# A one-layer language-model tower: the prologue's lists in another order, and VectorE's select of an expert unit ahead of the maximum

## The reference

```python
h = embeddings[x]                                   # one-hot product
n = layernorm(h)
q, k, v = n @ w_qkv  # 16 heads of 16; q and k are rotated (rope)
h = h + softmax(q @ k.T * 16 ** -0.5) @ v @ w_proj
y = layernorm(h)
e = argmax(y @ gate_w.T)                            # one of 8 experts per token
out = h + y + y @ expert_w[e].T
```

## Time and profile before

| | |
|---|---|
| median of 3 runs | 310.07 us (309.95 to 310.33) |
| profiled execution | 309.91 us, span 308.1 us |
| TensorE busy | 280.6 us, 91% |
| VectorE busy | 246.1 us, 80% |
| ScalarE busy | 132.8 us, 43% |
| GpSimd busy | 84.6 us, 27% |
| mean granted TensorE clock | 0.989 |

### The profile page before, as it was taken

The page is one execution under the profiler, slowest core; times in us unless marked ns, Lnnn a source line. Parts: engine busy times, 40 slices in busy tenths (PEclk is TensorE's granted clock), DMA queues, the critical chain, the costliest instruction groups (busy, mean ns, idle before and its releaser), DMA issues.

```text
span 308.1 us, 5610 instructions
## 1 busy us (share of the span) xinstructions
PE 280.6 (91%) x2060; PEld 200.9 (65%) x2060; DVE 246.1 (80%) x602; ACT 132.8 (43%) x271; POOL 84.6 (27%) x96
## 2 busy tenths in 40 slices
PE   2878889898799999899998999899999999999895
PEld 2657656656566776577766776677666666667674
DVE  8797997688969699788987798779897874657765
ACT  3155427667655535353436442463543454331000
POOL 5735418254454023411231041301210210210210
PEclk9999995999999999999999999999999999999999
DMA  3430331912900750049001930166010010001010
GB/s 117 179 150 7 110 105 47 152 26 62 150 8 12 127 81 2 12 103 138 4 0 39 155 52 1 36 115 94 2 37 3 2 36 2 1 3 34 0 36 34
DMA packets 10803, 17.55 MB, mean 57 GB/s; under 512 B 2024, under 2 KB 4883, under 8 KB 10648
## 3 DMA queue, kind: packets, MB, share of 16 engines
q1 hardware_dynamic: 9988, 16.62, 26.4%
q0 software_dynamic: 768, 0.55, 0.7%
q10 hardware_dynamic: 20, 0.02, 0.0%
HBM read 5.30 MB, written 2.10 MB: 24 GB/s over the span
## 4 chain that ended last, share of the span: by engine, by line
PE 52%; DVE 30%; issue 8%; POOL 5%; ACT 4%; DVEq 0%; POOLq 0%
PE e_bank L473 14%; PE f_bank L473 7%; PE o_bank L638 7%; DVE neg_max L986 6%; DVE acc L1083 5%; PE t_pair L603 5%; PE s_pair L473 4%; POOL qk L394 3%; PE m_bank L473 3%; PE s_pair L573 2%; PE m_bank L652 2%; DVE rope_a L969 2%; DVE rope_b L973 2%; ACT probs L850 2%; DVE xn L951 1%
## 5 line engine op out<-in xcount | busy, mean ns | idle before, releaser
L850 ACT ACTIVATE probs<-t_pair 128x512 f32<-128x512 f32 x128 | 69.6, 595 | 85.1 <-PE t_pair L603 84.6
L986 DVE TENSOR_REDUCE neg_max<-s_pair 128x2 f32<-128x512 f32 x128 | 81.9, 682 | 13.7 <-PE s_pair L573 13.5
L573 PE MATMUL s_pair<-stacks 48*128 48x256 f32 x256 | 49.4, 314 | 1.0 <-DVE neg_max L986 0.7
L603 PE MATMUL t_pair<-stacks 50*128 50x256 f32 x256 | 47.5, 313 | 1.9 <-DVE neg_max L986 1.4
L603 PEld LDWEIGHTS t_pair<-stacks 50*128 50x128 f32 x256 | 33.6, 189 | 23.8 <-issue 21.4
L473 PE MATMUL e_bank<-ew_h,y_h 128*128 128x512 f32 x92 | 40.3, 438 | 4.6 <-DVE acc L1079 2.7
L1083 DVE SCALAR_TENSOR_TENSOR acc<-e_bank,mask,acc 128x256 f32<-128x256 f32 x66 | 28.8, 478 | 11.2 <-PE e_bank L473 10.7
L573 PEld LDWEIGHTS s_pair<-stacks 48*128 48x128 f32 x256 | 34.6, 189 | 3.5 <-DVE neg_max L986 2.1
L473 PE MATMUL e_bank<-ew_l,y_h 128*128 128x512 f32 x92 | 36.4, 396 | 0.0
L473 PE MATMUL e_bank<-ew_h,y_l 128*128 128x512 f32 x92 | 36.2, 394 | 0.0
L394 POOL TENSOR_TENSOR qk<-rope_a,rope_b 128x512 f32<-128x512 f32 x16 | 20.6, 1294 | 54.2 <-DVE rope_b L973 54.2
(11 more groups left out here) (174 smaller groups left out, 536.6 us busy)
## 6 DMA issues: line engine op xcount, KB each, us to landing
stacks<-parts SPq DMA_DIRECT2D x36, 256.0 KB, 6.2
ew_raw<-in_expert_w SPq DMA_DIRECT2D x1, 2048.0 KB, 8.2
out<-res SPq DMA_DIRECT2D x7, 256.0 KB, 2.1
stacks<-parts SPq DMA_DIRECT2D x12, 128.0 KB, 2.9
probs<-in_w_qkv SPq DMA_DIRECT2D x2, 384.0 KB, 3.7
stacks<-max_rows SPq DMA_DIRECT2D x30, 8.0 KB
h<-in_emb,ids POOLq DMA_INDIRECT x16, 2.6
probs<-in_w_proj SPq DMA_DIRECT2D x1, 256.0 KB, 2.8
```

Source lines behind the costliest of these rows:

```text
L573: m = mm(s_pair[:, half, t * N:(t + 1) * N], stacks[b % STACKS][r:r + KS, pair, 0, t * P:(t + 1) * P], stacks[b % STACKS][r:r + KS, pair, ...
L603: m = mm(t_pair[:, half, c * N:(c + 1) * N], stacks[b % STACKS][r:r + KM, pair, 1, c * P:(c + 1) * P], stacks[b % STACKS][r:r + KM, pair, ...
L850: nc.scalar.activation(probs[:, (2 * v + half) % RING, :, :].rearrange("p c n -> p (c n)"), t_pair[:, half, :], ACT.Exp, scale=SCALE).then ...
L986: v.tensor_reduce(neg_max[:, k // 4, :, 4 * half + k % 4], s_pair[:, half, :].rearrange("p (t n) -> p t n", t=NT), AX.X, ALU.max, negate=T ...
```

## The change

On VectorE the select of a unit stands at the head of its slot, ahead of the maximum of that slot. In the prologue, VectorE makes f_norm_a(1) and x_low(0) ahead of the memsets of vals, subtracts y_l (x_low(1)) ahead of the z list and turns z_low and z_again round; the memsets of the ones column come last. ScalarE copies two z banks of the second tile (s_pair) ahead of two of the first, and the values of v later. GpSimd gathers batch 3 before it splits weights. TensorE's v projections are cut in two and moved behind visits 3 to 6, both transposes of batch 1 come a visit sooner, the first transpose of maxima goes into t_pair (`first_max_transpose`), one chunk of q and k moves behind visit 0 of step 0, and the fills there change from 2 ahead of step 0 and 1 after each of its visits to 3 after visit 0, 4 after visit 1 and 1 after each of the others.

```diff
@@ -219,7 +219,7 @@
             return (y_h[0], y_l[0]) if k == 1 else (x_h, x_l)
 
         Z_BANKS = [[m_bank, o_bank, f_bank, e_bank], [s_bank[0], s_bank[1], m_bank, o_bank]]
-        Z_ORDER = [(t, q) for t in range(NT) for q in range(4)]
+        Z_ORDER = [(0, 0), (0, 1), (1, 0), (1, 1), (0, 2), (0, 3), (1, 2), (1, 3)]
 
         def z_copied(t, q):
 
@@ -455,9 +455,9 @@
             rotated_sum(1, 0)
             rotated_sum(1, 1)
             f_rs_of(2)
+            gather(3)
             gate_weights()
             proj_weights_low()
-            gather(3)
             steps(step)
 
 
@@ -491,18 +491,21 @@
                         m = tr(x_bank(b)[:, k:k + P], xn[:, t, c * P:(c + 1) * P], ident[:, :])
                 m.then_inc(xt_ps, 1)
 
-            def project_v(b):
-                if b >= 2:
+            def project_v(b, tiles=range(NT)):
+                if tiles[0] > 0:
+                    pass
+                elif b >= 2:
                     wait(pe, qkl_ok, (b - 1) * NT + NT)
                 elif b == 1:
                     wait(pe, v_ok, b)
                 else:
                     pe.wait_ge(z_in, z_copied(1, 3))
                 x_h, x_l = x_parts(b)
-                for t in range(NT):
+                for t in tiles:
                     m = product(v_bank(b)[:, t * D:(t + 1) * D], lambda c: x_h[:, c, t, :], lambda c: x_l[:, c, t, :],
                                 lambda c: wqkv_h[:, c, 2 * D:3 * D], lambda c: wqkv_l[:, c, 2 * D:3 * D])
-                m.then_inc(v_ps, 1)
+                if tiles[-1] == NT - 1:
+                    m.then_inc(v_ps, 1)
 
             def project_qk(b, t, parts=range(C)):
                 if parts[0] > 0:
@@ -575,10 +578,19 @@
                 if t == NT - 1:
                     m.then_inc(s_ps, 1)
 
+            def first_max_transpose():
+
+                pe.wait_ge(roped, 2 * 2 * NT)
+                pe.wait_ge(ml_ok, 1)
+                for t in range(NT):
+                    m = tr(t_bank[1][0:16, N + t * P:N + (t + 1) * P].bitcast(F32R),
+                           max_parts[:, 0, t, :, :, :].rearrange("p i a j -> p (i a j)"), ident_r[:, :])
+                m.then_inc(mt_ps, 1)
+
             def max_transpose(b, u):
 
                 wait(pe, o_ok, (b - 1) * GROUPS + (4 if u else 2))
-                if b == 0 and u == 0:
+                if b == 0:
                     pe.wait_ge(v_ok, 2)
                 wait(pe, ml_ok, b * 2 + u + 1)
                 for t in range(NT):
@@ -712,8 +724,11 @@
                     g_at = SLOTS * b + s
                     if s % 2 == 0:
                         visit(b, s // 2)
+                        if b == 0 and s == 0:
+                            project_qk(2, 1, [1])
+                            pe.wait_ge(xl_ok, 3)
                         if b == 0:
-                            fill(m_bank, 1)
+                            fill(m_bank, 3 if s == 0 else 4 if s == 2 else 1)
                     if here(b, 0) and s == 3:
                         max_transpose(b, 1)
                     if here(b, 1) and s == maxima_slot(b + 1):
@@ -772,25 +787,24 @@
             project_qk(1, 1)
             z_transpose(1)
             visit(-1, 0)
-            project_v(0)
+            qk_transpose(1, 0)
             visit(-1, 1)
-            qk_transpose(1, 0)
+            qk_transpose(1, 1)
             visit(-1, 2)
-            qk_transpose(1, 1)
             x_transpose(2)
             visit(-1, 3)
-            project_v(1)
+            project_v(0, [0])
+            first_max_transpose()
             visit(-1, 4)
-            max_transpose(0, 0)
+            project_v(0, [1])
             project_qk(2, 0, [0])
             visit(-1, 5)
+            project_v(1, [0])
             project_qk(2, 0, [1])
             visit(-1, 6)
+            project_v(1, [1])
+            visit(-1, 7)
             project_qk(2, 1, [0])
-            visit(-1, 7)
-            project_qk(2, 1, [1])
-            pe.wait_ge(xl_ok, 3)
-            fill(m_bank, 2)
             steps(step)
 
 
@@ -834,7 +848,8 @@
 
             def max_row(b, u):
                 wait(act, mt_ps, b * 2 + u + 1)
-                copy(max_rows[:, u, :], o_bank[0:16, N:2 * N]).then_inc(mt_ok, 1)
+                turned = t_bank[1] if b == 0 and u == 0 else o_bank
+                copy(max_rows[:, u, :], turned[0:16, N:2 * N]).then_inc(mt_ok, 1)
                 if b == 0 and u == 0:
                     act.wait_ge(mt_ok, 1)
                     for half in range(2):
@@ -920,13 +935,13 @@
             for t, q in Z_ORDER:
                 z_copy(t, q)
             qk_high(1, 0)
-            values(0)
             qk_high(1, 1)
             qk_high_again(1, 0)
             qk_high_again(1, 1)
             x_high(2)
+            max_row(0, 0)
+            values(0)
             values(1)
-            max_row(0, 0)
             steps(step)
 
 
@@ -1105,6 +1120,8 @@
             def step(b, p):
                 for s in range(SLOTS):
                     g_at = SLOTS * b + s
+                    if here(b, -2) and s > 0 and unit_in(b, s - 1) is not None:
+                        select(b - 2, p, unit_in(b, s - 1), expert_banks(b - 2))
                     if here(b, 1) and s % 2:
                         maximum(b + 1, s // 2)
                         if s == 7:
@@ -1116,8 +1133,6 @@
                             g_norm_a(k)
                     for k in batches(post, "g_norm", g_at):
                         g_norm_b(k)
-                    if here(b, -2) and s > 0 and unit_in(b, s - 1) is not None:
-                        select(b - 2, p, unit_in(b, s - 1), expert_banks(b - 2))
                     for k in batches(front, "stats", g_at):
                         f_norm_a(k)
                     for k in batches(front, "norm", g_at):
@@ -1157,23 +1172,23 @@
             f_norm_b(0)
             dve.wait_ge(ident_ok, 1)
             v.tensor_copy(ident_r[:, :], ident[:, :]).then_inc(identr_ok, 1)
+            f_norm_a(1)
+            x_low(0)
             for i in range(VALS):
                 v.memset(vals[i][:, :, :, HD:STRIP], 0.0).then_inc(h_zero, 1)
-            x_low(0)
-            f_norm_a(1)
+            f_norm_b(1)
+            rotate(0, 0)
+            rotate(0, 1)
+            x_low(1)
+            z_low(0)
+            z_again(0)
+            z_low(1)
+            z_again(1)
+            rotate(1, 0)
+            rotate(1, 1)
             dve.wait_ge(h_zero, NB + VALS)
             for i in range(VALS):
                 v.memset(vals[i][:, :, :, HD:HD + 1], 1.0).then_inc(filled, 1)
-            f_norm_b(1)
-            rotate(0, 0)
-            rotate(0, 1)
-            z_again(0)
-            x_low(1)
-            z_low(0)
-            z_again(1)
-            z_low(1)
-            rotate(1, 0)
-            rotate(1, 1)
             maximum(0, 0)
             f_norm_a(2)
             maximum(0, 1)

```

## The result

The changed kernel takes 366.23 us (median of six runs, 362.92 to 366.38) where the kernel before, on the same chip, takes 310.2 (309.0 to 313.93). The ratio is 1.176, 95% interval 1.170 to 1.182. The forecast was 352.0: the direction and the kind of loss are as forecast, the size is 14 us short, and the time lies at the upper end of the range, inside it by 0.8 us.

What follows compares the result with a forecast made beforehand. TensorE, busy 91%, was taken as the bound, losing time where it must wait for VectorE. 309.9 + 36.8 (waits) - 2.0 (prologue) + 7 (clock falls) = 351.7, taken as 352 us; range 334 to 367.

Steps and rivals of the forecast that it cites:

- E: Passage between steps, steps 3 to 5: select 7 to unit 1 takes 9.91 us, before 7.00; +2.91 each.
- A: Unit 3 of every step and unit 7 of step 5, almost directly before a visit: 2.68 us, before 0.96; +1.72.
- B: Second strips' transpose needing o_n, after unit 1, and unit 2 in step 6: 2.79 us, before 1.66; +1.13.
- C: Transpose of yn, behind the maximum of visit 5: 2.80 us; +1.58 in steps 2 to 4, +2.01 in 5 and 6.
- The sum of 36.8: Steps 2 to 6: added waits of TensorE for VectorE over all five kinds of place, 36.8 us; bounds 18 and 41.
- D: Gate needing y_l, behind the maximum of visit 6, steps 5 and 6: 2.76 us, before 1.67; +1.09.
- The covered places: After units 4, and units 2 and 6 in steps 2 to 4: some 2.3 us of TensorE work covers VectorE, no cost.
- 3 falls at 2.3: TensorE's clock falls to half once at each passage in steps 3 to 5: 7 us together, ends 0 and 23.
- the first rival: Clock falls behind A and C too, ten falls at 2.3 us in steps 2 to 6: 368 us; chance 0.15.
- Forecast -2.0: Prologue: subtracting y_l before the z list copy saves 2.0 us until the first maximum; bounds 0.7 and 2.4.
- Half absorbed: Unseen slack takes half of the 36.8 and the clock stays up: 326 us, 335 with two thirds kept; chance 0.13.
- Not slower: Select first frees e_bank sooner, ending 2.7 us of waits, with prologue and clock savings: 302 us; chance 0.03.

Runs made afterwards that it cites:

- the kernel with fills: The changed kernel with 106 extra matmuls into free banks where TensorE would stand waiting in steps 2 to 6: 351.4 us, ratio 1.125.
- the kernel with A alone: The kernel before with the select ahead of the maximum only at unit 3 of steps 2 to 6: 322.04 us, ratio 1.033.
- the select alone: The kernel before with only the select moved ahead of the maximum in its slot, the prologue left old: 368.85 us, ratio 1.173.
- only the covered units: The kernel before, select first only at unit 4 (steps 2 to 6), unit 2 (2 to 5), unit 6 (2 to 4): 314.99 us, ratio 1.005.
- place E alone: The kernel before, select first only at unit 7 of steps 2 to 4 and unit 0 of steps 3 to 5: 325.63 us, ratio 1.049.

## Why the prediction came out as it did

**The mechanism: right.** VectorE stands in the select, the maximum queues behind it, the visit waits for the maximum. Most signs came: 29.1 us of such waits (20 to 30 said), y_l at 18.00 (within 19 said), gaps above a microsecond behind units 3 and 5 of every step. Two did not: the PEclk digits are 7 to 9 in the loop and not 5, and all ahead of step 2 and the tail are not as before but 2.8 and 1.2 us longer.

**The prices from the unit's end: right to hundredths.** E: select 7 at 174.22, unit 1 at 184.14, so 9.92 (9.91 said). A: the unit ends at 153.70 and the next starts at 156.39, 2.69 (2.68). B: 187.07 to 189.86, 2.79 (2.79). C: 206.01 to 208.82, 2.81 (2.80). What counts there are VectorE's durations; TensorE's clock is at half for only 0.4 us of B and 0.1 of E. What I had wrong in E is how TensorE spends the time: visit 1 starts at 183.10, 8.88 after select 7, as said, but TensorE is ready for it at 6.25 and not at 5.5, so its gap is 2.63 us, not 3.4.

**The sum of 36.8: right, in part by luck.** With the clock at full it is 36.3. From unit to unit in the kernel with fills, against the kernel before, A cost 1.71 (1.72 said), B 1.20 (1.13 said; 0.73 in step 2, the "smaller B" that I had left out), D 1.15 (1.09) and E 2.92 (2.91). C cost 1.97 in steps 5 and 6 (2.01 said), but 1.20 in steps 2 to 4 (1.58 said): the transposes of yn start 1.59 later, but the next unit follows them after 0.41 us where it was 0.79 (changed kernel, step 4; kernel before, step 3). So step 2 cost 3.9 (4.43 said) and steps 3 and 4 7.0 each (7.34). Against that stand 0.56 at unit 0 of step 6 (in the changed kernel, at full clock), which I had left out, and 0.25 at unit 0 of step 2. The errors cancel. The covered places, priced at nothing, cost nothing.

**The clock: the step that failed.** I took 3 falls at 2.3, 7 us. There were nine, at 1.4 each, 12.9 us. The count failed: I had expected falls only behind E; they came behind all three E, behind A in steps 3, 5 and 6, behind the gaps of 1.54 us at C in steps 5 and 6, and behind one of 1.11 us in step 6. The price failed too: I had taken it from a fall of 6.8 us at half rate, and eight of the nine last 3.4 us. So the first rival had the count (ten), and its price of 2.3 was too high by 0.9. Why not behind A in steps 2 and 4, with the same 1.66 us gap? The runs do not settle this; that the clock sometimes falls behind a gap of one length and sometimes does not is seen again in the kernel with A alone, and in the one with the select alone, where it falls behind A of step 2 too. The Trainium skill's rule that I had weighed (TensorE: Matmul & The Clock Gate, section "HAM oscillation — how this bites in real kernels"), that waits between bursts can throw the clock back each time round a loop, deserved more than the weight of 0.15 that I gave it: the trace agrees in four of five steps, all but step 2. The page's own case has waits for DMAs that are longer than any gap here (2.63 us at most), so it does not say which of the short ones count.

**The prologue: wrong by some 5 us.** Forecast -2.0, found +2.8 in the profile. The start gained 1.3 of the 2.0 said (first visit at 25.34, before 26.65). The part that I could not price and put at nothing, with +4 as one end, was +4.1: the new TensorE list by itself at least 1 us, the rest the clock's longer stretch at half rate (PEclk 65 in place of one 5; 13.7 us for 6.8). How much of the 5 us one sees depends on the execution that one compares with, since the old prologue stands at half rate for 13.7 us too in the profiled executions of "only the covered units" and "place E alone". By the medians the new prologue changes nothing (1.001), which is 2 us off the forecast. VectorE's list alone is the faster one (0.994).

**The check.** 309.9 + 36.3 + 12.9 + 2.8 + 1.2 for the tail is 363.1; the profiled execution took 363.12. Select 0 of step 4 came 18.1 us later, not 13: 4.8 from the prologue and 1.0 from two falls in step 3 (3.3) in place of one at 2.3, less the 1.0 that steps 2 and 3 cost under their forecast. The tail's 1.2 also stands in the kernel with fills and not in those with only A or E; I have not traced it. The median lies 3.1 us above it with a lower clock: two executions of 362.9 and 363.1 have 0.934 over the span, the four of 366.2 to 366.4 have 0.925. So the clock's part of the median is, by estimate, some 16 us, over twice what I forecast; no execution of 366 us was profiled. That the median still lies in the range is luck of 0.8 us: the select alone, at 368.85, is outside.

**The other rivals.** Half absorbed (326 to 335): no, with the clock held the sum comes whole. Not slower: no; the e_bank waits of 2.7 us are gone, but longer waits for a maximum stand in their place.

## What to carry to other kernels

Price a wait by the sum of what stands in the queue ahead of the awaited result, from the event that releases the queue: done place by place, that sum came out within 2%, with errors of 0.2 to 0.6 us at single places that cancelled. Ask also what else stands behind the work that is delayed: a place that is covered by itself made the next one 0.4 to 0.6 us longer. An in-order engine should do the work whose input is there before the work whose input is still being made, even if the latter frees a buffer.

Then ask separately what the new gaps do to TensorE's clock, count the gaps of a microsecond too and not only the longest, and price a fall from a step with it and one without it (here 1.3 to 1.6 us). Where a gap can't be removed, matmuls into a free bank that fill it can pay at once, but no more than fit the gap (ten where 0.66 us were free cost 1.4 us): 366 to 351 us with fills in the loop here, and in the prologue, together with VectorE's new list, 1.2% below the kernel before with a spread of half a microsecond.

## What the runs showed of the hardware

The kernel before is not one time but several: 308.75 to 315.57 us on one chip, in step with the granted clock over its span: 0.993 at 308.8, 0.988 at 310.2, 0.972 at 313.7, 0.967 at 315.6. With VectorE's new list and nine more matmuls, six executions agree within 0.52 us and the clock is at 0.998 or more.

A gap's length alone does not say whether the clock falls. In one and the same execution it fell behind 1.66 us in step 3 and not in steps 2 and 4, and behind 1.11 us in step 6 but not behind 1.10 us in steps 2 to 4. Behind 2.00 us in the prologue of the kernel before it did not fall. And it fell with no such gap: in the changed kernel's prologue it is at half from 30.45 us on, although no gap between 20.9 and 30.4 us is longer than 0.36; several short ones left TensorE busy 2.51 of the last 3.40 us:

```profile
27.00:30.40 3.40, 2.51 (x15) 1.63 (x14) 3.40 (x10) 2.36 (x5) 2.02 (x3) 1.00 0.04 14
```

The copy that took 1.45 us beside GpSimd's sum takes 0.41 in its new place, after those sums. With that the trace agrees with the exclusive lock of the Trainium skill (SBUF — State Buffer, section "SBUF: two separate sides") that the prediction weighed:

```profile
20.10 0.41 DVE L1104 CAST stacks<-qk 128x256 fp32r<-128x256 f32 x1
```
